# Turning the row sums of a graph kernel with VectorE blocks and small DMAs instead of TensorE

## What is computed

```python
h = jnp.maximum(_layernorm(x, axis=-1), 0.0)
eye = jnp.zeros_like(A1) + jnp.eye(N, dtype=A1.dtype)
shifted = jnp.roll(eye, 1, axis=0)
A_fwd = [A1, A2, shifted]                       # A1 = A2 = adj
A_list = A_fwd + [jnp.swapaxes(a, 1, 2) for a in A_fwd]
A_list.append(eye)
A = jnp.stack(A_list, axis=0)
HW = jnp.einsum('bnf,rfo->rbno', features, W[:, :F]) \
   + jnp.einsum('rd,rdo->ro', W_edges, W[:, F:])[:, None, None, :]
AHW = jnp.einsum('rbnm,rbmo->rbno', A, HW)
out = jnp.max(AHW, axis=0) + b
return x + out                                  # features = h
```

## Time and profile before

| | us |
|---|---|
| time before, median of 3 runs | 216.8 |
| lowest and highest run | 215.47, 218.54 |
| the profiled execution, its own time | 217.13 |
| span of its trace | 215.1 |
| mean granted TensorE clock | 0.991 of full speed |

### The profile page before, as it was taken

How to read it: one execution, slowest core, us unless ns; L and a number is a source line. 1 busy time by engine, 2 the same in 40 slices (tenths; PEclk the granted TensorE clock), 3 DMA queues, 4 the chain that set the end, 5 groups by cost and what they waited for, 6 DMA issues and landing times.

```text
span 215.1 us, 3407 instructions
## 1 busy us (share of the span) xinstructions
PE 205.6 (96%) x900; PEld 148.9 (69%) x900; DVE 176.9 (82%) x416; ACT 161.2 (75%) x433; POOL 89.0 (41%) x140
## 2 busy tenths in 40 slices
PE   7998699999999999999999999999999999999992
PEld 7456367767767777777767767776777777777771
DVE  3485987999889797988979798888979798897755
ACT  3888919897896969698796969689696969876230
POOL 3042633627252542726163452725254372726200
PEclk9999969999999999999999999999999999999999
DMA  6999999797595959789494968859395958824101
GB/s 182 307 347 376 365 320 257 167 362 197 192 369 141 387 102 355 222 265 318 158 388 84 402 148 317 267 195 369 101 406 121 375 146 257 279 98 52 50 0 49
DMA packets 33747, 51.06 MB, mean 237 GB/s; under 512 B 1873, under 2 KB 11329, under 8 KB 33729
## 3 DMA queue, kind: packets, MB, share of 16 engines
q1 hardware_dynamic: 31152, 46.53, 62.5%
q0 software_dynamic: 2304, 4.20, 11.9%
q10 hardware_dynamic: 272, 0.13, 0.2%
HBM read 46.65 MB, written 4.19 MB: 236 GB/s over the span
## 4 chain that ended last, share of the span: by engine, by line
PE 78%; DVE 8%; DMA 5%; SPq 4%; issue 2%; ACT 1%; DVEq 0%; ACTq 0%
PE bank_p L816 11%; PE bank_p L818 9%; PE bank_p L817 9%; PE bank_g L776 6%; PE bank_gT L755 5%; DMA x_sb<-in_x_dram 5%; PE bank_g L780 5%; PE bank_g L781 5%; PE bank_g L787 5%; PE bank_gT L767 4%; PE bank_gT L761 4%; PE bank_gT L760 4%; DVE best L613 3%; PE bank_p L806 3%; PE bank_p L716 3%; PE bank_p L724 3%
## 5 line engine op out<-in xcount | busy, mean ns | idle before, releaser
L323 POOL TENSOR_TENSOR a_lo<-adj_sb,a_hi 128x512 fp32r<-128x512 f32 x15 | 19.5, 1303 | 66.7 <-DVE h_lo L582 57.7
L613 DVE TENSOR_TENSOR best<-bank_p,best 128x512 f32<-128x512 f32 x48 | 33.2, 691 | 8.0 <-PE bank_p L818 6.9
L610 DVE SCALAR_TENSOR_TENSOR best<-bank_p,c_col,best 128x512 f32<-128x512 f32 x32 | 24.0, 750 | 9.2 <-ACT best L457 8.7
L438 ACT ACTIVATE gT_hi<-bank_gT 128x512 fp32r<-128x512 f32 x16 | 9.5, 594 | 28.8 <-PE bank_gT L767 28.3
L393 ACT ACTIVATE a_hi<-adj_sb 128x512 fp32r<-128x512 f32 x45 | 27.7, 621 | 0.0
L406 ACT ACTIVATE aT_hi<-adjT_sb 128x512 fp32r<-128x512 f32 x45 | 27.7, 621 | 0.0
L422 ACT ACTIVATE h<-x_sb,shift,rstd 128x128 f32<-128x128 f32 x60 | 24.7, 489 | 1.1 <-DVE shift L562 1.1
L780 PE MATMUL bank_g<-aT_hi,h_hi 128*128 128x512 f32 x45 | 24.4, 543 | 0.0
L576 DVE TENSOR_TENSOR aT_lo<-adjT_sb,aT_hi 128x512 fp32r<-128x512 f32 x30 | 24.1, 841 | 0.0
L760 PE MATMUL bank_gT<-a_hi,h_hi 128*128 128x512 f32 x45 | 23.6, 525 | 0.0
L309 POOL DMA_DIRECT2D x_bias<-in_xT_dram x16 | 13.9, 872 | 23.2 <-DMA x_bias<-in_biasT_dram 23.2
(11 more groups left out here) (118 smaller groups left out, 510.4 us busy)
## 6 DMA issues: line engine op xcount, KB each, us to landing
adj_sb<-in_adj_dram SPq DMA_DIRECT2D x15, 1024.0 KB, 5.7
adjT_sb<-in_adjT_dram SPq DMA_DIRECT2D x15, 1024.0 KB, 6.4
x_bias<-in_biasT_dram SPq DMA_DIRECT2D x16, 256.0 KB, 5.9
x_bias<-in_xT_dram POOLq DMA_DIRECT2D x16, 256.0 KB, 4.8
x_sb<-in_x_dram SPq DMA_DIRECT2D x15, 256.0 KB, 7.8
out_dram<-o_sb SPq DMA_DIRECT2D x15, 256.0 KB, 5.8
adj_sb<-in_adj_dram SPq DMA_DIRECT2D x4, 256.0 KB, 5.6
adjT_sb<-in_adjT_dram SPq DMA_DIRECT2D x4, 256.0 KB, 5.4
```

The costliest lines, as they stand in the source:

```text
L613: op = nc.vector.tensor_tensor(best[q][:, :], product, best[q][:, :], ALU.max)
```

## The change

For batches 0 and 1 the sums go as before. From batch 2 (`TURNED`) on, TensorE's four identity matmuls, ScalarE's copy and GpSimd's `part_sums` are gone. In their place VectorE makes 32 columns a node (`sum_cols`: direction, copy, hi or lo, chunk) and turns them in blocks of 32 x 32 (`sum_blocks`); this is done at the head of iteration b, behind `take_best(b-1, 6)`. SyncE, at the head of its iteration b, stores the 128 x 32 block to a DRAM scratch (16 KB), waits until it has landed, and issues four loads of 4 rows of 2 KB each, gathered from 64 pieces of 128 bytes, into the four groups of `sumsT`, which is now double. `begin_products(b)` waits for these. The core of the diff:

```diff
@@ sync
+            def turn_sums(b):
+                i = b - TURNED + 1
+                q = b % 2
+                sp.wait_ge(blocks_turned, i)
+                sp.dma_start(scratch, sum_blocks[:, :]).then_inc(scratch_in, 16)
+                sp.wait_ge(scratch_in, 16 * i)
+                sp.wait_ge(prod_psum, (b - 1) * NPROD)
+                for g in range(len(ORDER_A)):
+                    sp.dma_start(sumsT[q][g * GROUP:g * GROUP + 4, :].rearrange("r (c j s) -> r c j s", c=C, s=GROUP)
+                                 .bitcast(F32), scratch_rows[g // 2]).then_inc(sumsT_in[q], 16)
             for b in range(1, B):
+                if b >= TURNED:
+                    turn_sums(b)
                 if b + 3 < B:
                     load_x(b + 3)
@@ gpsimd
                     split_adjT_last(b + 1)
-                    part_sums(b + 1)
@@ scalar, split_adj
-                if b >= 2:
+                if 2 <= b < 2 + TURNED:
                     act.wait_ge(parts_lo, b - 1)
+                elif b >= 2 + TURNED:
+                    act.wait_ge(cols_lo, b - 1 - TURNED)
@@ scalar, the loop
                 split_g(b)
-                copy_sumsT(b)
+                if b < TURNED:
+                    copy_sumsT(b)
                 begin_best(b)
@@ vector
+            def turn_blocks(b):
+                q = b % 2
+                i = b - TURNED + 1
+                s = sums[q][:, :, :].unsqueeze(2).to_broadcast([P, 2, 2, C])
+                dve.wait_ge(sums_ready, 2 * b + 2)
+                nc.vector.tensor_copy(sum_cols[:, :, :, 0, :], s).then_inc(cols_hi, 1)
+                dve.wait_ge(cols_hi, i)
+                nc.vector.tensor_tensor(sum_cols[:, :, :, 1, :], s, sum_cols[:, :, :, 0, :].bitcast(F32),
+                                        ALU.subtract).then_inc(cols_lo, 1)
+                dve.wait_ge(cols_lo, i)
+                if i >= 2:
+                    dve.wait_ge(scratch_in, 16 * (i - 1))
+                nc.vector.transpose(sum_blocks[:, :], sum_cols[:, :, :, :, :].rearrange("p d k s c -> p (d k s c)")
+                                    .bitcast(F32)).then_inc(blocks_turned, 1)
             for b in range(2, B):
+                turn_blocks(b)
                 if b + 2 < B:
                     variance(b + 2)
@@ tensor, begin_products
-                pe.wait_ge(sumsT_ready, b + 1)
+                if b < TURNED:
+                    pe.wait_ge(sumsT_ready, b + 1)
+                else:
+                    pe.wait_ge(sumsT_in[b % 2], 64 * (b // 2))
@@ tensor, the loop
                 aggregate(b)
-                turn_sums(b)
+                if b < TURNED:
+                    turn_sums(b)
```

More of the change, by code:

```diff
@@ L27 @@
 WARM_UP = 9
+TURNED = 2
 NX = 4
 def gnn_kernel(nc: bass.Bass, x: bass.AP, xT: bass.AP, adj: bass.AP, adjT: bass.AP, W: bass.AP,
-               W_rel: bass.AP, W_edges: bass.AP, biasT: bass.AP, outT: bass.AP):
+               W_rel: bass.AP, W_edges: bass.AP, biasT: bass.AP, outT: bass.AP, scratch: bass.AP):
     B, N, F = x.shape
@@ L44, in gnn_kernel @@
     w_dram = W[:, :F, :].rearrange("r f o -> f r o")
+    scratch_rows = scratch.rearrange("(j d r c) s -> d r c j s", d=2, r=4, c=C)
     with ExitStack() as ctx:
@@ L83, in gnn_kernel @@
         sum_parts = pair("sum_parts", [P, C, 2, 2, GROUP], F32R)
-        sumsT = sb("sumsT", [P, N], F32R)
+        sumsT = pair("sumsT", [P, N], F32R)
+        sum_cols = sb("sum_cols", [P, 2, 2, 2, C], F32R)
+        sum_blocks = sb("sum_blocks", [P, GROUP])
         x_bias = pair("x_bias", [P, N])
@@ L179, in gnn_kernel @@
         sumsT_ready = sem("sumsT_ready")
+        cols_hi = sem("cols_hi")
+        cols_lo = sem("cols_lo")
+        blocks_turned = sem("blocks_turned")
+        scratch_in = sem("scratch_in")
+        sumsT_in = [sem(f"sumsT_in{i}") for i in range(2)]
         hT_psum = sem("hT_psum")
@@ L293, in part_sums @@
                 pool.wait_ge(sums_ready, 2 * b + 2)
-                if b >= 2:
-                    pool.wait_ge(sumsT_psum, b - 1)
                 for copy in range(2):
@@ L447, in copy_sumsT @@
                 act.wait_ge(sumsT_psum, b + 1)
-                if b >= 1:
-                    act.wait_ge(prod_psum, b * NPROD)
-                nc.scalar.activation(sumsT[:, :], bank_s[:, 0:N], ACT.Copy).then_inc(sumsT_ready, 1)
+                nc.scalar.activation(sumsT[b % 2][:, :], bank_s[:, 0:N], ACT.Copy).then_inc(sumsT_ready, 1)
             def begin_best(b):
@@ L796, in begin_products @@
                 for i in range(NH, NPROD - int(b == B - 1)):
-                    add_sums(i, bank_of[i], start=True)
+                    add_sums(b, i, bank_of[i], start=True)
                 if b == B - 1:
@@ L800, in begin_products, with add_sums @@
                     for nodes, to in zip(HALVES, last_banks):
-                        add_sums(NPROD - 1, to, nodes, start=True)
-            def add_sums(i, to, nodes=slice(0, N), start=False, stop=False):
+                        add_sums(b, NPROD - 1, to, nodes, start=True)
+            def add_sums(b, i, to, nodes=slice(0, N), start=False, stop=False):
                 group = ORDER_A.index(ORDER[i])
                 rows = slice(group * GROUP, (group + 1) * GROUP)
-                return nc.tensor.matmul(to[:, nodes], c_rows[rows, :], sumsT[rows, nodes], start=start, stop=stop)
+                return nc.tensor.matmul(to[:, nodes], c_rows[rows, :], sumsT[b % 2][rows, nodes], start=start, stop=stop)
             def passes(i, dst, nodes=slice(0, N), start=False, stop=False):
@@ L826, in product @@
                     pe.wait_ge(wlo_ready, 1)
-                if i == 2:
+                if i == 2 and b < TURNED:
                     pe.wait_ge(sumsT_ready, b + 1)
@@ L849, in products_first @@
                 for i in range(NH, NPROD):
-                    add_sums(i, bank_of[i], stop=True).then_inc(prod_psum, 1)
+                    add_sums(0, i, bank_of[i], stop=True).then_inc(prod_psum, 1)
             pe.wait_ge(ident_ready, 1)
@@ L899 @@
     args.append(nc.dram_tensor("out_0_dram", (batch, features, nodes), F32, kind="ExternalOutput").ap())
+    args.append(nc.dram_tensor("scratch_dram", (P, GROUP), F32, kind="Internal").ap())
     gnn_kernel(nc, *args)
```

## The result

The changed kernel takes 240.5 us (median of 4 runs, 237.1 to 242.1) against 216.6 us before: 1.104 times as long, 95% interval 1.098 to 1.111. The forecast was 218, with a range up to 226. The sign of case B's small loss was right, the size was not: 24 us were added, not one.

A forecast was written before the change was run, and what follows sets the result against it. TensorE was taken to bound the kernel, then the DMA queue loop: 216.8 less 5.8 removed, plus 7.6 for twelve loop periods less 0.7 of cover, gives 217.9, so 218 us; 8-in-10 range 210.5 to 226.

The forecast's parts named there:

- case B: Main forecast: the loop through SyncE's DMA queue sets the period at 12.1 to 12.9 us, 218 us; chance 0.42.
- What is removed: TensorE's identity matmuls leave the chain: 0.41 us a batch, 5.8 us over fourteen batches, period 11.87 us.
- case A: Rival: everything added is hidden and the loop closes in 11.9 us or less, 211.0 us; chance 0.24.
- VectorE's work: Three small added operations on VectorE take 0.6 us a batch, hidden with 0.3 us to spare.
- The way of the sums: Store, wait and four loads on SyncE's queue: store 2.2 us, sumsT there at t = 7.85, cover 0.65 us.
- The loop through the DMA queue: Scratch store can't pass adjT on SyncE's queue: 12.5 us from one store landing to the next, above 11.87.
- S: Landing of the scratch store, put at 3.85 us after the batch's start on TensorE, from 3.4 to 5.4.
- The accumulation: The bias's accumulating transfer, 144 packets, 1.5 us, sharing the DMA engines: loop 13.4 us with a third, 14.4 with all.
- Hidden, by 2 us: GpSimd's late bias: add_bias 1 to 2 us behind the batch's start, split_adjT_last ending by t = 4, reader at 6.1.
- It just fits: adj, issued 3.1 us later behind SyncE's wait, lands at t = 12.0 to 12.3; ScalarE needs it by 12.5.
- D: Rival: latency alone too long, store 2.7 and gathers 3.7 us to land, period 12.9, 224.4 us; chance 0.12.
- C: Rival: slower, queue loop over 12.77 us as the accumulating transfer meets store and gathers; 226.3 us at 13.2; chance 0.22.

The follow-up runs named there:

- the store-only kernel: Changed kernel with the scratch store and SyncE's wait for it kept, but the four gathers not issued (that part left out): 228.2 us.
- the early turn: Changed kernel with VectorE turning the next batch's blocks ahead of the fifth maximum of this one, transfers unmoved: 238.0 us, ratio 1.099.

## Why the prediction was wrong, step by step

**What is removed: right.** 0.41 us a batch was forecast, and without the transfers the period is 11.85 where 11.87 was named, 210.3 us where case A had 211.0.

**VectorE's work: right.** Three operations, from 110.93 to 111.48 in batch 7:

```profile
110.93 0.16 DVE L628 CAST sum_cols<-sums 128x16 fp32r<-128x16 f32 x1
...
111.13 0.18 DVE L630 TENSOR_TENSOR sum_cols<-sums,sum_cols 128x16 fp32r<-128x16 f32 x1
...
111.34 0.21 DVE L635 STREAM_TRANSPOSE sum_blocks<-sum_cols 128x32 f32<-128x32 f32 x1
```

**The way of the sums: too dear when free, too cheap when not.** I took 2.2 us for the store. With idle engines it is 1.4, and in the loaded kernel 5.1. The upper bound of 3.7 from w_edge was too low for a store behind a whole `adjT`.

**The loop through the DMA queue: the right mechanism, the wrong size.** This is the step that failed: the loop is the term that was mis-sized. From S to `adj`'s issue I had 2.4 us; measured are 3.3 (86.81 to 90.10), since a gather holds the queue for 0.66 with its gap and not 0.48: I took the issue time of the big loads for a shape that no row showed. From `adj`'s issue to `adjT`'s landing I had 9.6 and 0.5 for `x`; measured are 10.7 in this batch (90.10 to 100.8) and 11.0 on average. The loop is 14.1 here and 14.5 in the mean of twelve, and not 12.5. With 14.5, the prediction's own sum is 12 x 2.6, less 5.8 and 0.7, on top of 216.8, which is 241.5 for a profiled execution of 242.1: this one term holds the whole error. The bounds of 12.0 to 13.4 (14.4 with the whole accumulation) were too low as well. The accumulation is not the reason: in this batch a third of it, 48 of 144 packets, falls into the stretch, 8.5% of 10.7 us, just what the 13.4 allowed for. The issue of the gathers gives 0.9 us of the 2.0; what makes up the other 1.1, `x` included, was not taken apart.

**"Hidden, by 2 us": this step failed in its logic.** I moved GpSimd's work by the delay of the bias and asked only who reads its results. I didn't ask what GpSimd's running does to VectorE at the new time. Before, GpSimd's subtraction ran beside the maxima; after, it runs beside VectorE's work on SBUF, and operations of 0.16 us take up to 2.8 in the store-only kernel. This gives a second loop of 13.3 us there. In the changed kernel the queue loop hides it; it shows as soon as that loop is cut (228.2 and 233.4 us). The step was not right for GpSimd's own reader either: in the changed kernel the last matmuls of `aggregate` (L826) waited for `split_adjT_last` seven times, 5.8 us in all. And a late bias can close a third loop, over SyncE's store of the output, which costs the kernel before 12 us.

**"It just fits" for `adj`: wrong.** It had to land by t = 12.5 and was reckoned at 12.3. ScalarE waited for it in 12 batches, 50.1 us in total. The 5.5 us of landing became 7.2 (median). (The reckoning itself should read 11.75 to 12.25: 6.25 + 5.5 or 6.0.) It is a second arm of the same loop, and not the one that bound: no landing of `adj` stands in the chain's line above.

**The rivals.** D is out by the early turn. C, a long loop, is what happened: its point of decision, 12.77 us, was passed by far. Its chance of 0.22 stood below that of B, and the one value worked out for it (226.3 at a loop of 13.2) is 14 us short. The reason it gave, the accumulation meeting store and gathers, is a small part of the loop. The queue's order, which I held for the reason, is only part of it: a queue of its own didn't let the store pass.

## What to carry to other kernels

A small transfer that a queue must wait for is not priced by its own latency but by what the engines have ahead of it, and by all that stands behind the wait on the issuing queue; write down the loop from one wait to the next, with each issue in it, before adding one. Two such loops can lie a microsecond apart: removing one then gains only the distance to the other, which is no proof against it. When a step slides in time, check not only who reads its result but also what runs beside it at the new place; on VectorE and GpSimd that is worth microseconds.

## What the runs showed of the hardware

A 16 KB store from SBUF to DRAM lands in 1.4 us when nothing bulky is under way, and in 4.9 and 5.4 us (medians of the two kernels) while bulk loads drain, though it is alone on ScalarE's queue; one of 2 KB still needs 4.7. Why it can't pass is open.

An issue of a gather of 64 pieces of 128 bytes holds SyncE's queue for 0.61 us (median, 0.60 to 0.78), where the 1 MB load of `adj` took 0.37.

VectorE's block transposition of 128 x 32 fp32 in blocks of 32 x 32 takes 0.21 us, in every batch.

After TensorE's idle time of 1.84 us the granted clock fell to its lower level of 1.2 GHz, and matmuls came every 0.43 us in place of 0.23. By stretch (the third number from the end is the clock):

```profile
103.00:105.10 2.10, 0.29 (x2) 0.00 (x0) 2.06 (x5) 2.10 (x9) 1.27 (x1) 1.00 0.16 36
105.10:108.70 3.60, 3.57 (x11) 2.69 (x12) 1.24 (x3) 0.20 (x2) 0.00 (x0) 0.57 0.98 282
```

In these 3.6 us the clock was granted at 0.57 of full speed. That made this batch's products some 1.6 us longer. The store behind them was issued at 111.58 and landed at 114.4 with `adjT`, so the queue loop hid the loss here.
